# Causal attention with a routed low-rank layer on one core: value blocks issued ahead of the turn's scores

## Chip, core and metric

One core of a Trainium2 chip runs the whole kernel in one launch. The metric is the device time in microseconds; the table below has the median of three runs.

## What is computed

One sequence of 2048 rows of width 128 goes through one layer: layer norm, attention with 16 heads of width 8, and, after a second layer norm, a base product, a shared low-rank branch and six routed low-rank experts of rank 16, of which each row keeps its best two.

```python
qkv = x @ w_qkv                                   # x: [1, 2048, 128], layer-normed
q, k = _apply_rope(q, cos, sin), _apply_rope(k, cos, sin)
scores = jnp.einsum('bhqd,bhkd->bhqk', q, k) * dh ** -0.5
scores = jnp.where(causal, scores, finfo.min)
attn = jax.nn.softmax(scores, axis=-1)
x = x + jnp.einsum('bhqk,bhkd->bhqd', attn, v) ... @ w_out
h = _layernorm(x)
base_out = h @ base_W.T + base_b
shared_out = (h @ shared_A.T) @ shared_B.T
sparse_w = the two largest of softmax(h @ router_W.T + router_b), renormalised
x = x + base_out + shared_out + routed_out        # experts weighted by sparse_w
```

## The kernel before, in words

The attention is computed with scores transposed: keys lie on the partitions, queries on the free dimension. The 16 heads form four groups of four. The queries are cut into six pieces (`PIECES`: 2, 2, 4, 4, 2, 2 tiles of 128), and a piece of one head group is a **group** of work: 24 groups, 23 boundaries between them. For each group the keys are walked from the first to the diagonal.

A **unit** is what fills one score buffer `ps` of 128x1024 (two banks): two heads by 512 queries ("full"), or four heads by 256 ("wide"), with trimmed forms on the diagonal ("ends", "mid", "half"). There are 280 units, and `NS` = 3 score buffers. In the order of units:

- TensorE computes the scores of unit u (`scores`, line 1029) once the exponential of unit u-3 has freed the buffer (line 1020).
- ScalarE takes the exponential of all of it in one instruction (line 625) into one of `NPB` = 8 buffers `pbuf`.
- GpSimd zeroes what lies above the diagonal (line 575), for diagonal units alone.
- TensorE multiplies by the values (`values`, line 1052) into the one accumulator `po`, whose ninth column per head sums the exponentials. This is done by **blocks**, mostly of two units: 145 blocks, block b due `LAG` = 5 turns after its last unit (`blocks_by_unit`). Turns with and without a due block mostly alternate; a unit of kind "mid" is a block by itself and shifts the alternation.
- At a group's last block VectorE transposes `po` out (`evacuate`, line 685), in the block's turn; TensorE's first block of the next group waits for that (line 1048).

Everything else is cut into **jobs**, whose turns are a table (`ORDER`, `PLACES`): T turns normalised rows, Q, K (QS, KS) and V are projections, B is a bound on the scores, and O, X, R, U, F are the output product and the second half of the layer for a chunk of up to four tiles. Each job's product goes through the one bank `pm` and is taken by VectorE (`take`) before the next may start (line 1087). F is two runs of matmuls (lines 1062 and 1119). The rows of the input are prepared in five steps (`PREPS`: 2, 2, 4, 4, 4 tiles) and finished in five (`FINISHES`: 4, 4, 4, 2, 2); for T, Q, K, V and B "chunk n" is the n-th preparation, for O, X, R, U and F the n-th finish, from 0. Where the text names a job it gives the turn: F of chunk 0 is at turn 75, of chunk 1 at 144, of chunk 2 at 199, of chunk 3 (two tiles only) at 253.

Each engine runs its instructions in the order written. TensorE's order is that of the loop at lines 1228 to 1247: in turn u the waits for new keys and queries, then the unit's scores, the filler matmuls of the first four turns, the due block's values, and the jobs. In what follows S, E and V with a number are the scores of a unit, the exponential of a unit, and the values of a block, all counted from 0.

Of the kernel before, what the change touches and what calls it, by code (L numbers as in the profile page):

```python
# [121 lines left out]
def blocks_by_unit():  # L122


    due = {}
    for b, block in enumerate(BLOCKS):
        due.setdefault(block["units"][-1] + LAG, []).append(b)
    return due


def pieces(unit_kind):

    return {"full": [(0, 0, CH, 0)],
            "ends": [(0, P, CH - P, 0), (2, CH - P, P, CH - P)],
            "mid": [(0, 2 * P, 2 * P, 0)],
            "wide": [(0, 0, 2 * P, 0)],
            "half": [(0, P, P, 0)]}[unit_kind]


def pair_step(unit_kind):  # L140

    return P if unit_kind == "half" else 2 * P


def value_terms(block):


    kind = UNITS[block["units"][0]]["kind"]
    terms = []
    for u in block["units"] if kind in ("wide", "half", "mid") else block["units"][:1]:  # L150
        kt, step = UNITS[u]["kt"], pair_step(UNITS[u]["kind"])
        for dk, q0, n, place in pieces(UNITS[u]["kind"]):
            if len(UNITS[u]["pairs"]) == 2:
                sources = [(u, (j % 2) * CH + (j // 2) * step) for j in range(GH)]
            else:
                sources = [(block["units"][j // 2], (j % 2) * CH + place) for j in range(GH)]
            terms.append((kt + dk, q0, n, sources))
    return terms
# [64 lines left out]
def build(nc, x, w_qkv, rope_c, rope_s, w_out, w_down, w_up, w_base, router_b, ident, head_sum,  # L223
# [3 lines left out]
    with ExitStack() as ctx:  # L227
# [196 lines left out]
        def side(stacked, e):  # L424

            return stacked[e * SIDE:(e + 1) * SIDE]
# [7 lines left out]
        def wait_for_fill(engine, p):  # L434

            engine.wait_ge(filled, FILLS_BY_ACT[chunk(p)])
            if FILLS_BY_POOL[chunk(p)]:
                engine.wait_ge(filled_by_pool, FILLS_BY_POOL[chunk(p)])

        def wait_for_keys(engine, p):  # L440

            engine.wait_ge(keys_in[p], 16 * len(SLOTS))

        def wait_for_queries(engine, p):

            if p == 0:
                engine.wait_ge(queries_in[0], 16 * (len(SLOTS) - len(FIRST_BY_POOL) - len(FIRST_BY_ACT)))
                engine.wait_ge(queries_by_pool, 16 * len(FIRST_BY_POOL))
                engine.wait_ge(queries_by_act, 16 * len(FIRST_BY_ACT))
            else:  # L450
                engine.wait_ge(queries_in[p], 16 * len(SLOTS))
# [83 lines left out]
        def _(pool):  # L535
# [23 lines left out]
            for u, unit in enumerate(UNITS):  # L559
                if u in LATE_FILL_UNITS:  # L560
                    stacked, value, tile = LATE_FILLS[LATE_FILL_UNITS.index(u)]
                    fill(kst if stacked == "K" else qst, value, tile, 1)
                if not unit["diagonal"]:
                    continue
                pool.wait_ge(exp_ready, u + 1)
                buf = pbuf[:, u % NPB, :]
                if unit["kind"] in ("mid", "wide"):
                    edges = [buf.rearrange("p (h q) -> p h q", h=4)[:, :, 0:P]]
                elif unit["kind"] == "half":
                    edges = [buf[:, e * CH:e * CH + 2 * P].rearrange("p (h q) -> p h q", h=2) for e in range(2)]  # L570
                else:
                    heads = buf.rearrange("p (h q) -> p h q", h=2)
                    edges = [heads[:, :, place:place + P] for _, _, _, place in pieces(unit["kind"])]
                for edge in edges:
                    ins = nc.gpsimd.affine_select(out=edge, in_=edge, compare_op=ALU.is_ge, fill=0.0, base=0,  # L575
                                                  pattern=[[0, edge.shape[1]], [1, P]], channel_multiplier=-1)
                ins.then_inc(masked, 1)
# [436 lines left out]
        def _(pe):  # L1014
            def scores(u):

                unit = UNITS[u]
                i, g, kt = unit["i"], unit["g"], unit["kt"]
                if u >= NS:
                    pe.wait_ge(exp_ready, u - NS + 1)  # L1020
                if u == 2:
                    pe.wait_ge(second_read, 2)
                for at, pair in enumerate(unit["pairs"]):
                    for dk, q0, n, place in pieces(unit["kind"]):
                        key = (kt + dk) * P
                        q = PIECES[i][0] * P + q0
                        place += at * pair_step(unit["kind"])
                        for e in range(2):
                            ins = nc.tensor.matmul(ps[:, u % NS, e, place:place + n],  # L1029
                                                   side(kst, e)[:, g * 2 + pair, key:key + P],  # L1030
                                                   side(qst, e)[:, g * 2 + pair, q:q + n], start=True, stop=True)
                ins.then_inc(scores_ready, 1)

            def values(b):

                blk = BLOCKS[b]
                last_unit = blk["units"][-1]
                i, g = blk["i"], blk["g"]
                if blk["diagonal"]:
                    pe.wait_ge(masked, MASKS_THROUGH[last_unit])  # L1040
                    pe.wait_ge(v_ready, max(p for at, p in NEW_PREP.items() if at <= i) + 1)
                else:
                    pe.wait_ge(exp_ready, last_unit + 1)
                if blk["first"]:
                    group = i * NG + g
                    pe.wait_ge(v_ready, 2)
                    if group:
                        pe.wait_ge(o_free, group)
                terms = value_terms(blk)
                for m, (kt, q0, n, sources) in enumerate(terms):  # L1050
                    for j, (u, at) in enumerate(sources):
                        ins = nc.tensor.matmul(po[32 * j:32 * j + DH + 1, q0:q0 + n],  # L1052
                                               va[:, kt, g * GH + j, :], pbuf[:, u % NPB, at:at + n],
                                               start=blk["first"] and m == 0,
                                               stop=blk["last"] and m + 1 == len(terms), skip_group_check=True)
                ins.then_inc(block_done, 1)
# [107 lines left out]
            def keep_warm(times, left, right, into=ps[:, 1, 1, :]):  # L1164

                for _ in range(times):
                    nc.tensor.matmul(into, left, right, start=True, stop=True)  # L1167
# [59 lines left out]
            due = blocks_by_unit()  # L1227
            for u in range(len(UNITS)):
                if u in FIRST_UNIT and FIRST_UNIT.index(u) in NEW_PREP:
                    p = NEW_PREP[FIRST_UNIT.index(u)]  # L1230
                    row_maxima(p)
                    wait_for_fill(pe, p)
                    if p == 0:
                        keep_warm(WARM_KEYS, *hot)
                    wait_for_queries(pe, p)
                if u in NEW_KEYS_UNIT:
                    wait_for_keys(pe, NEW_KEYS_UNIT[u])
                scores(u)
                if u < len(WARM_UNITS):
                    keep_warm(WARM_UNITS[u], *hot, pm[:, :])  # L1240
                for b in due.get(u, ()):
                    values(b)
                for n in JOBS_AT.get(u, ()):
                    job(n)
            for u in range(len(UNITS), len(UNITS) + LAG):
# [59 lines left out]
```

## Time and profile before

| what | us |
|---|---|
| median of 3 runs | 309.06 |
| lowest and highest run | 307.85, 311.37 |
| the profiled execution, whole | 307.79 |
| its span, first to last instruction | 306.0 |

The granted TensorE clock was 0.999 of full over the span. A timeline row gives the start in us from the span's start, how long the row's instructions took together, and how many they are (x8); consecutive instructions of one kind are merged. In brackets is the idle time of the engine just before, and what ended it. A row's length includes the draining of its last matmul, so where the next group of TensorE starts is the better measure of what a group costs. Full score groups have two matmuls of 512 columns, wide ones four of 256; a row x4 or x8 can hold two units.

### The profile page before, as it was taken

The numbers are of one execution on the slowest core, as the hardware profiler recorded it, in microseconds if no ns is written. First come the engines' busy times: TensorE is split into PE (matmuls) and PEld (weight loads), VectorE is DVE, ScalarE is ACT, GpSimd is POOL, SyncE is SP. The second block draws the span as 40 slices with busy tenths as digits, with TensorE's granted clock in tenths as the row PEclk, the third lists the DMA queues.
The fourth block names the chain that finished last, engine by engine and source line by source line (L and its number), as shares of the span: only waits on it lengthen the run. The fifth ranks groups of instructions, "written<-read, shape, count | busy, mean of one in ns | idle before, by whom it ended". The sixth has DMA issues, their size and how long they took to land.

```text
span 306.0 us, 7517 instructions
## 1 busy us (share of the span) xinstructions
PE 280.3 (92%) x3008; PEld 101.9 (33%) x3008; DVE 143.4 (47%) x424; ACT 266.2 (87%) x300; POOL 64.0 (21%) x140
## 2 busy tenths in 40 slices
PE   7867887898999899899999999999999999998995
PEld 2613242221423322123324113443533333433352
DVE  6875594689756467936341003761000524101064
ACT  8646597889899789999999999999999999999910
POOL 3673146505032102203012030101101010103000
PEclk9999999999999999999999999999999999999999
DMA  6423147003520100330000100000000000000000
GB/s 206 117 69 95 27 106 209 1 3 81 150 80 2 37 0 1 103 105 2 2 1 2 35 2 2 2 3 0 28 10 3 2 2 0 2 19 2 3 0 17
DMA packets 15704, 11.75 MB, mean 38 GB/s; under 512 B 2081, under 2 KB 14738, under 8 KB 15666
## 3 DMA queue, kind: packets, MB, share of 16 engines
q1 hardware_dynamic: 15170, 10.90, 12.8%
q8 instruction: 25, 0.41, 0.6%
q10 hardware_dynamic: 432, 0.20, 0.3%
q0 software_dynamic: 64, 0.13, 0.2%
q14 instruction: 13, 0.11, 0.1%
HBM read 3.88 MB, written 1.05 MB: 16 GB/s over the span
## 4 chain that ended last, share of the span: by engine, by line
PE 32%; ACT 26%; DVE 21%; issue 16%; DMA 2%; DVEq 1%; SPq 0%; ACTq 0%
ACT pbuf L625 26%; PE po L1052 14%; PE ps L1029 8%; PE pm L1068 3%; DVE rest L703 3%; DVE rot L710 2%; DVE absmax L734 1%; DVE rot L697 1%; DVE rest L720 1%; PE pm L1062 1%; PE pm L1105 1%; DVE parts L727 1%; DVE parts L718 1%; DMA xs<-x_dram 1%; DVE parts L729 1%
## 5 line engine op out<-in xcount | busy, mean ns | idle before, releaser
L625 ACT ACTIVATE pbuf<-ps 128x1024 f32<-128x1024 f32 (+1 forms) x280 | 253.7, 1087 | 21.3 <-PE ps L1029 20.7
L1052 PE MATMUL po<-pbuf,va 128*9 128x256 f32 (+3 forms) x1792 | 143.8, 426 | 4.2 <-DVE oq L685 2.6
L1029 PE MATMUL ps<-qst,kst 64*128 64x256 bf16 (+3 forms) x896 | 96.2, 297 | 6.1 <-ACT pbuf L625 2.1
L575 POOL TENSOR_SCALAR_AFFINE_SELECT pbuf<-pbuf 128x256 f32<-128x256 f32 (+1 forms) x104 | 48.7, 490 | 207.4 <-ACT pbuf L625 205.6
L1029 PEld LDWEIGHTS ps<-qst,kst 64*128 64x128 bf16 x896 | 29.8, 94 | 100.6 <-ACT pbuf L625 75.7
L1052 PEld LDWEIGHTS po<-pbuf,va 128*9 128x9 f32 x1792 | 35.2, 89 | 59.2 <-issue 35.0
L685 DVE STREAM_TRANSPOSE oq<-po 128x256 f32<-128x256 f32 (+1 forms) x24 | 12.9, 539 | 82.2 <-PE po L1052 80.8
L1167 PE MATMUL ps<-kst 128*128 128x512 bf16 x46 | 11.3, 380 | 0.8 <-issue 0.8
L703 DVE TENSOR_TENSOR rest<-pm,sinT 32x512 f32<-32x512 f32 x16 | 11.0, 687 | 0.3
L1068 PE MATMUL pm<-xnT,wqkv 128*128 128x512 f32 x16 | 9.0, 644 | 1.9 <-DVEq L850 1.9
L652 DVE BATCH_NORM_STATS2 stats<-xs 128x6 f32<-128x128 f32 x32 | 7.1, 281 | 2.9 <-DMA xs<-x_dram 1.4
L844 DVE COPY lowT<-pm 113x512 f32<-113x512 f32 (+1 forms) x4 | 2.5, 624 | 12.5 <-PE pm L1115 12.5
L847 DVE TENSOR_TENSOR xs<-pm,xs 128x512 f32<-128x512 f32 (+1 forms) x4 | 2.5, 626 | 11.8 <-PE pm L1119 11.8
L817 DVE TENSOR_TENSOR xs<-pm,xs 128x512 f32<-128x512 f32 (+1 forms) x4 | 2.5, 625 | 9.4 <-PE pm L1105 9.4
L1167 PE MATMUL ps<-xnT 128*128 128x512 bf16 x16 | 5.3, 504 | 1.5 <-DVE xnT L962 1.5
L1167 PEld LDWEIGHTS ps<-kst 128*128 128x128 bf16 x46 | 4.3, 99 | 5.3 <-issue 1.7
L1080 PE MATMUL pm<-hsum,bnd 128*1 128x16 f32 x10 | 1.0, 177 | 5.5 <-DVEq L850 4.4
L710 DVE TENSOR_TENSOR rot<-rot,rest 128x512 f32<-128x512 f32 (+1 forms) x10 | 5.9, 586 | 0.3
L539 POOL MEMSET qst<- 128x512 f32 (+1 forms) x9 | 6.0, 684 | 0.0
L583 ACT COPY kst<-fillers 128x2048 f32<-128x2048 f32 x3 | 5.7, 1896 | 0.0
L720 DVE TENSOR_TENSOR rest<-rot,parts 128x512 f32<-128x512 f32 (+1 forms) x8 | 5.5, 694 | 0.3
L697 DVE TENSOR_TENSOR rot<-pm,cosT 128x512 f32<-128x512 f32 x4 | 2.8, 691 | 5.6 <-PE pm L1068 5.1
(150 smaller groups left out, 183.6 us busy)
## 6 DMA issues: line engine op xcount, KB each, us to landing
qst<-parts SPq DMA_DIRECT2D x18, 128.0 KB, 2.4
kst<-parts SPq DMA_DIRECT2D x18, 128.0 KB, 2.5
xs<-x_dram SPq DMA_DIRECT2D x4, 256.0 KB, 3.5
cosT<-rope_c_dram SPq DMA_DIRECT2D x3, 256.0 KB, 3.9
sinT<-rope_s_dram SPq DMA_DIRECT2D x3, 256.0 KB, 4.3
kst<-parts SPq DMA_DIRECT2D x12, 64.0 KB, 2.1
out_dram<-xs SPq DMA_DIRECT2D x3, 256.0 KB, 2.3
qst<-parts SPq DMA_DIRECT2D x7, 64.0 KB, 2.0
```

What stands on the lines that cost most here:

```text
L539: nc.gpsimd.memset(stacked[:, :, first * P:(first + tiles) * P].bitcast(F32), value).then_inc(filled_by_pool, 1)
L575: ins = nc.gpsimd.affine_select(out=edge, in_=edge, compare_op=ALU.is_ge, fill=0.0, base=0, pattern=[[0, edge.shape[1]], [1, P]], channel_ ...
L625: nc.scalar.activation(probs[:, :, 0:width], ps[:, u % NS, :, 0:width], ACT.Exp, scale=SCALE).then_inc(exp_ready, 1)
L652: ins = nc.vector.bn_stats(stats[:, t, :], xs[:, tile + t, :])
L685: nc.vector.transpose(oq[:, g, mine, :].rearrange("p b r -> p (b r)"), po[:, 0:nt * P]).then_inc(o_free, 1)
L703: ins = nc.vector.tensor_tensor(rest[there:there + HALF, which, cols], product[here:here + HALF, :], sinT[here:here + HALF, c % 2, cols], ...
L710: return nc.vector.tensor_tensor(rot[:, which, cols], rot[:, which, cols], rest[:, which, cols], ALU.add)
L720: then(nc.vector.tensor_tensor(rest[:, which, cols], rot[:, which, cols], parts[:, which, 0, cols], ALU.subtract))
L1029: ins = nc.tensor.matmul(ps[:, u % NS, e, place:place + n], side(kst, e)[:, g * 2 + pair, key:key + P], side(qst, e)[:, g * 2 + pair, q:q ...
L1052: ins = nc.tensor.matmul(po[32 * j:32 * j + DH + 1, q0:q0 + n], va[:, kt, g * GH + j, :], pbuf[:, u % NPB, at:at + n], start=blk["first"] ...
L1068: return nc.tensor.matmul(product, wqkv[:, which, :], xnT[:, chunk(p) % 2, local(p)], start=True, stop=True)
L1167: nc.tensor.matmul(into, left, right, start=True, stop=True)
```

## The change

In a unit's turn the values of the due block are issued ahead of the scores instead of behind them. The jobs stay behind the scores. The waits move with their instructions, and the block due in a turn stands behind the waits for new keys and queries. The orders on VectorE, ScalarE, GpSimd and SyncE are as before.

```diff
                 if u in NEW_KEYS_UNIT:
                     wait_for_keys(pe, NEW_KEYS_UNIT[u])
+                for b in due.get(u, ()):
+                    values(b)
                 scores(u)
                 if u < len(WARM_UNITS):
                     keep_warm(WARM_UNITS[u], *hot, pm[:, :])
-                for b in due.get(u, ()):
-                    values(b)
                 for n in JOBS_AT.get(u, ()):
                     job(n)
```

TensorE around the first group boundary after unit 76, before: V39 (9x256, the last of its group), S81 and S82, V40 (the first of the next), S83 and S84, V41, and T of chunk 4.

```order
L1052 MATMUL po<-pbuf,va 9x256 x4
L1029 MATMUL ps<-qst,kst 128x512 x4
L1052 MATMUL po<-pbuf,va 9x512 x4
L1029 MATMUL ps<-qst,kst 128x512 x4
L1052 MATMUL po<-pbuf,va 9x512 x4
L1095 MATMUL pm<-idf,xn 128x128 x4
L1029 MATMUL ps<-qst,kst 128x512 x4
```

Now, from V39 on:

```order
L1052 MATMUL po<-pbuf,va 9x256 x4
L1029 MATMUL ps<-qst,kst 128x512 x4
L1052 MATMUL po<-pbuf,va 9x512 x4
L1029 MATMUL ps<-qst,kst 128x512 x4
L1052 MATMUL po<-pbuf,va 9x512 x4
L1029 MATMUL ps<-qst,kst 128x512 x2
L1095 MATMUL pm<-idf,xn 128x128 x4
```

The rows between V39 and V40 read alike, but they are S80 and S81 now: S82 and S83 stand behind V40. T, in turn 84, now has one score group between itself and V41.

TensorE around the bound B of chunk 4 in turn 102, before: V50 (the last of its group), S102, B, S103, V51.

```order
L1052 MATMUL po<-pbuf,va 9x256 x4
L1029 MATMUL ps<-qst,kst 128x512 x2
L1080 MATMUL pm<-hsum,bnd 1x16
L1029 MATMUL ps<-qst,kst 128x512 x2
L1052 MATMUL po<-pbuf,va 9x512 x4
```

Now V50 is followed by S101 and S102:

```order
L1052 MATMUL po<-pbuf,va 9x256 x4
L1029 MATMUL ps<-qst,kst 128x512 x4
L1080 MATMUL pm<-hsum,bnd 1x16
L1052 MATMUL po<-pbuf,va 9x512 x4
L1029 MATMUL ps<-qst,kst 128x512 x4
```

S103 has moved behind V51, which waits for the transposition.

TensorE around F of chunk 2 in turn 199, before: V100, S199, F, S200, V101.

```order
L1052 MATMUL po<-pbuf,va 9x256 x8
L1029 MATMUL ps<-qst,kst 128x256 x4
L1062 MATMUL pm<-wbase,feat 128x128 x4
L1119 MATMUL pm<-wup,lowT 128x128 x4
L1029 MATMUL ps<-qst,kst 128x256 x4
L1052 MATMUL po<-pbuf,va 9x256 x8
```

Now V100 is followed by S198 and S199:

```order
L1052 MATMUL po<-pbuf,va 9x256 x8
L1029 MATMUL ps<-qst,kst 128x256 x8
L1062 MATMUL pm<-wbase,feat 128x128 x4
L1119 MATMUL pm<-wup,lowT 128x128 x4
L1052 MATMUL po<-pbuf,va 9x256 x8
L1029 MATMUL ps<-qst,kst 128x256 x4
```

F and V101 are now between S199 and S200, where F alone was.

## Rows read from the trace of the kernel before

**Rows 1.** The page, part 1: busy us (share of span) xinstructions

```profile
PE 280.3 (92%) x3008; PEld 101.9 (33%) x3008; DVE 143.4 (47%) x424; ACT 266.2 (87%) x300; POOL 64.0 (21%) x140
```

**Rows 2.** Table of waits, whole span: us in total, times, longest us

```profile
PEld ps L1029 <- ACT pbuf L625: 75.7, 140, 0.9
ACT pbuf L625 <- PE ps L1029: 20.7, 25, 2.9
PE po L1052 <- DVE oq L685: 2.6, 4, 1.4
```

**Rows 3.** Timeline, 180:200: start, us, engine, instructions [idle before <-releaser]

```profile
179.11 21.82 ACT L625 ACTIVATE pbuf<-ps 128x1024 f32<-128x1024 f32 x24
190.17 1.16 PE L1105 MATMUL pm<-wout,feat 128*128 128x128 f32 x8
191.26 0.39 PE L1029 MATMUL ps<-qst,kst 64*128 64x256 bf16 x4
191.58 1.05 PE L1052 MATMUL po<-pbuf,va 128*9 128x256 f32 x16
192.57 0.61 PE L1029 MATMUL ps<-qst,kst 64*128 64x256 bf16 x8
193.11 1.05 PE L1052 MATMUL po<-pbuf,va 128*9 128x256 f32 x16
```

**Rows 4.** Timeline, 101 to 110 us, after F of chunk 0 and at a group's end

```profile
101.64 0.61 PE L1029 MATMUL ps<-qst,kst 64*128 64x512 bf16 x4
102.07 2.85 ACT L625 ACTIVATE pbuf<-ps 128x1024 f32<-128x1024 f32 x3 [1.89 <-PE ps L1029]
...
106.82 0.72 DVE L685 STREAM_TRANSPOSE oq<-po 128x512 f32<-128x512 f32 x1
107.68 1.04 PE L1052 MATMUL po<-pbuf,va 128*9 128x512 f32 x8 [1.39 <-ACT pbuf L625]
108.66 0.61 PE L1029 MATMUL ps<-qst,kst 64*128 64x512 bf16 x4
109.09 1.94 ACT L625 ACTIVATE pbuf<-ps 128x1024 f32<-128x1024 f32 x2 [0.50 <-PE ps L1029]
```

**Rows 5.** Timeline, 118 to 131 us: K of chunk 4 and the transposition after it

```profile
118.06 1.12 PE L1068 MATMUL pm<-xnT,wqkv 128*128 128x512 f32 x2
...
127.83 0.72 DVE L685 STREAM_TRANSPOSE oq<-po 128x512 f32<-128x512 f32 x1
127.99 0.39 PE L1029 MATMUL ps<-qst,kst 64*128 64x512 bf16 x2
130.11 1.03 ACT L625 ACTIVATE pbuf<-ps 128x1024 f32<-128x1024 f32 x1 [0.37 <-PE ps L1029]
```

**Rows 6.** Timeline, 217 to 222 us: F of chunk 2 in turn 199

```profile
215.42 3.94 ACT L625 ACTIVATE pbuf<-ps 128x1024 f32<-128x1024 f32 x4
217.06 0.39 PE L1029 MATMUL ps<-qst,kst 64*128 64x256 bf16 x4
217.38 1.16 PE L1062 MATMUL pm<-wbase,feat 128*128 128x128 f32 x8
219.36 0.39 PE L1029 MATMUL ps<-qst,kst 64*128 64x256 bf16 x4
219.80 1.03 ACT L625 ACTIVATE pbuf<-ps 128x1024 f32<-128x1024 f32 x1 [0.43 <-PE ps L1029]
221.00 1.51 ACT L625 ACTIVATE pbuf<-ps 128x512 f32<-128x512 f32 x2 [0.17 <-PE ps L1029]
```

**Rows 7.** Timeline, 58 to 63 us: T of chunk 3 and the exponential of unit 37

```profile
58.69 0.65 PE L1095 MATMUL pm<-idf,xn 128*128 128x128 f32 x4 [1.29 <-DVEq L850]
...
62.07 1.02 ACT L625 ACTIVATE pbuf<-ps 128x1024 f32<-128x1024 f32 x1 [1.33 <-PE ps L1029]
```

**Rows 8.** Groups on ScalarE, 100:120, then 120:140: busy, mean ns | idle

```profile
L625 ACT ACTIVATE pbuf<-ps 128x1024 f32<-128x1024 f32 x19 | 18.1, 1039 | 3.4 <-PE ps L1029 3.4
...
L625 ACT ACTIVATE pbuf<-ps 128x1024 f32<-128x1024 f32 x22 | 20.5, 1053 | 0.7 <-PE ps L1029 0.6
```

## Prediction, made before the changed kernel had run

> **What bounds the kernel now.** I read the busy shares first. TensorE is listed at 92% and ScalarE at 87% [rows 1], so neither is plainly the bound. The waits decide: TensorE's weight loads for scores wait 75.7 us in 140 waits for an exponential to free a score buffer, while ScalarE waits only 20.7 us, 25 times, for scores, and TensorE only 2.6 us, 4 times, for a transposition [rows 2]. So the exponentials set the pace nearly everywhere, and the timeline says how fast that is: 24 of them in 21.82 us, 0.91 us each [rows 3]. TensorE needs, for two units and their values, the values (0.99 us from 191.58 to 192.57) and two score groups (0.54, from there to 193.11), together 1.53 us, against 1.82 us of two exponentials [rows 3]. It is ahead by 0.3 us per pair, and a job (O: 1.09 us from 190.17 to 191.26) eats what it gained in four pairs.
>
> I number units 0 to 279 (scores S, exponentials E), blocks of values V 0 to 144; V40 is due at unit 82.
>
> **How much room a score has.** S(u) may start once E(u-3) has ended (I allow 0.1 us for the signal). From a score's start to its exponential's start is 0.43 us (108.66 to 109.09) and such an exponential lasts 1.02 us, as 219.80 with 1.03 shows again [rows 4, 6]. So S(u+1) must start 1.45 us before E(u+1) is due to end, that is at most 4 x 0.91 - 0.1 - 1.45 = 2.1 us after the earliest start of S(u). Between those two starts there is room for the score itself (0.32, from 191.26 to 191.58 [rows 3]) and 1.78 us more: values alone (0.99) or a job alone (1.09) fit; values and a job of 1.09 exceed it by 0.3 us; values and F (F was 217.38 to 219.36, 1.98 us [rows 6]) by 1.2 us. T (0.65 us [rows 7]) and jobs of its size (X, U) fit even with values.
>
> **What the change does.** No instruction is added or removed on any engine, and the orders of VectorE, ScalarE, GpSimd and SyncE, DMAs included, are as before. On TensorE each block of values passes one score group. Seen from the scores this moves the values one gap earlier; seen from the jobs it regroups: before, a job shared its gap with values when both are due in one turn; now, when values are due in the turn after the job. The sum is of what becomes of each such meeting. A block's masks and exponentials are of the unit five turns back and were ready one gap earlier too, so I put the value waits for them at nothing (ScalarE's E(u-4) has ended by then; if POOL were late the block would wait up to one mask).
>
> Up to unit 37 (62 us): 0. Jobs Q, QS and K stand in turns 9, 11 and 13 with values due in 10, 12 and 14, so three exponentials come a value block (0.8 us) later, and V10 now holds back S26. But the end of this stretch is set by VectorE: transposes T of chunk 3 start at 58.69 when its rows are ready, then Q, and E37 starts at 62.07 [rows 7], in both orders. ScalarE idled 1.33 us just before it; that swallows the lateness, at most one value block, that the exponentials carry until then. Bounds: 0 to +0.8.
>
> Units 37 to 83: +1.1 us. Again much is given back, at F of chunk 0: TensorE reaches S76 at 101.64 after an unbroken run of value, job and score [rows 4], and has the same work in front of it in the new order; I keep 0.2 for the wait before U. Then comes the first group boundary behind a long VectorE chain: V39 ends a group and V40 opens the next and must wait for the transposition, which ran from 106.82 to 107.54 because VectorE was on chunk 4's statistics. Before, S81 and S82 had been issued ahead of V40 (107.68; its row names ScalarE, but the transposition ended last) and only E83 was late, by 0.50 us. Now S82 stands behind V40: 107.68 + 0.2 + 0.98 = 108.86, E82 ends at 110.3, E83 at 111.2 against 109.09 + 1.02 = 110.1. So +1.1, of it 0.9 from this wait. Bounds: 0 (if VectorE comes earlier) to 1.9, two exponentials' worth.
>
> Units 84 to 94: 0. T, Q and K of chunk 4 are at turns 84, 86, 92 with values in the same turns. They are relieved, but TensorE arrives late and the walk ends as it began. With 0.32 and 0.21 per score, 0.98 per block, 0.65 for T and 1.05 for Q, K is issued at 118.8, not at 118.06 [rows 5]. Bounds: -1.0, the stalls of these three jobs (3.4 us of the stretch 100 to 120 less 1.89 and 0.50 [rows 4, 8]), to +0.5.
>
> Units 101 to 104: +0.5 us. VectorE's work on K ends 0.7 us later, so the transposition for V50 moves from 127.83 to 128.5 and V51 from 128.7 to 129.4. Before, S103 went ahead of it (127.99) and only E104 idled, 0.37 us [rows 5]. Now S103 starts at 130.4, E103 ends at 131.8, E104 at 132.7 against 131.14: +1.6 in all, 0.5 more than before this place. Bounds 0 to 1.1.
>
> The other meetings, in the room worked out above: V job at 109 relieved (idle 0.6 in the stretch 120 to 140, less 0.37 [rows 8]: about -0.1); O at 114 with V57: +0.3 less a stall that goes, +0.1; R at 127, O at 169, R at 179, and F at 253, which is half as long (two tiles): +0.3 each, 1.2 together; F at 199: 1.2 now and 0.2 for the next score, where before E200 ended at 220.83, 1.47 us after its forerunner at 219.36 (0.56 too late) and the next two 1.68 after it (0.28 too late, one being half as long, 0.49) [rows 6]: 1.4 - 0.84, +0.5; F at 144, which I take to have cost the same before, but where the next score follows 0.2 us behind without loss: 1.2 - 0.84, +0.3. Bounds of these together: 0 (all covered by the lead ScalarE has) to 3.5.
>
> Sum: 0 + 1.1 + 0 + 0.5 - 0.1 + 0.1 + 1.2 + 0.5 + 0.3 = +3.6 us. After unit 83 little can absorb it, since each exponential waits only for the one before, and the last value block waits for the last exponential. The profiled execution took 307.79 us (span 306.0), so it would be 311.4. The three runs shown have a median of 309.06, 1.3 above that execution; on them the forecast is 309.06 + 3.6 = 312.7, and I round it down to 312.5.
>
> A page gives another view of TensorE. By the Trainium skill (Perfetto Trace Analysis, section Identifying the Most-Contended Engine) matmul busy time is no measure of how near TensorE is to its limit, and weight-load busy time is one. That is 33% here [rows 1], so by that rule there would be room for any order, and the time would not change: 309.1. Against it stands the cycle of 1.53 us in 1.82 [rows 3]: five sixths of the time are taken, whatever the weight loads show.
>
> **Rivals.**
> No difference, 309.1 us (308.3 to 310.0): the lead hides the regrouping, as the 1.53 against 1.82 us would let it if no job came close. For it: only 20.7 us of waits in all. Against: F and O meetings are arithmetic on rows.
>
> Not slower, in fact faster, 307.9 us or less: values are now issued while the score waits for its buffer (75.7 us of such waits [rows 2]), so TensorE no longer idles first and lags afterwards. The jobs at 84, 86, 92, 109 and 114 lose their stalls, 1.0 + 0.2 = 1.2 us, and the new meetings cost nothing. It decides if values start more than about 0.3 us earlier than the old ones relative to the exponentials, which covers the excess of 0.3. To pass -1% the early stretch must give some of its idle time too. Against: F exceeds the room fourfold.
>
> Much slower, 319 us: there are 23 group boundaries, and at each the second score after the old group's last block is now behind the transposition (last values end, 0.1, transposition 0.45 to 0.72, first values 0.98). If 17 of them cost 0.6 us each, that is 10 us. Against: two score groups lie between the two value blocks in either order, and the table puts only 2.6 us down to it (V40's 1.39 us come on top).
>
> **Chances.** Forecast 0.50, no difference 0.25, faster-side rival 0.12, much slower 0.13. One per cent, 3.1 us, is about what a measurement of this kernel can tell; the forecast lies just above it. Of its half I put 0.37 above +1% and 0.13 below; of the faster rival 0.07 passes -1%. So faster 0.07, same 0.43, slower 0.50. The range, from the no-difference case's lower part to half way into the last rival, is 308.8 to 317.0; the forecast's own range is 309.8 to 315.5.
>
> **What would show it.** Right: E37 within 0.5 us of 62.07; E82 starting behind V40 and an idle of about 1 us before it; idle of about 1 us before E103, E145 and E200 instead of E104 and the halved pairs; VectorE and the tail (last exponential to end) unchanged in length; ScalarE's wait for scores up from 20.7 to some 24 us plus what the early part shifts. Wrong: if V40 does not hold S82, if the score after F and values follows within 2.2 us, or if the exponentials after 104 us are earlier than before.

## The result, and the profile after

The changed kernel took 312.17 us (median of 4 runs, 310.74 to 313.23) against 308.90 for the kernel before (4 runs, 307.85 to 311.37): 1.0106 times, with a 95% interval of 1.0066 to 1.0145. It is slower by 3.3 us, a third of a microsecond from the forecast of 312.5. The profiled execution took 310.74 us, its span 309.0, against 307.79 and 306.0 before. An execution that is over 1.5% above the fastest of its own kernel stands in no median and no ratio from here on. The agreement is better than the reasons behind it: the order of the instructions costs 2.0 us, not 3.6, and the rest is TensorE's clock, which the prediction did not treat.

The page's busy shares and its row of the granted clock, changed kernel:

```profile
PE 282.4 (91%) x3008; PEld 102.6 (33%) x3008; DVE 142.9 (46%) x424; ACT 266.4 (86%) x300; POOL 64.3 (21%) x140
...
PEclk9999999999999999899999999999999999999999
```

As many instructions as before [rows 1]; TensorE is busy 2.1 us longer with the same matmuls. The clock row has an 8 in its seventeenth slice, about 124 to 131 us.

The table of waits (engine, line, releaser: us in total, times, longest):

```profile
ACT pbuf L625 <- PE ps L1029: 23.9, 27, 3.1
...
PE po L1052 <- DVE oq L685: 3.4, 5, 1.8
```

ScalarE waits 3.2 us more for scores than before (20.7 [rows 2]): that is about the whole difference of the spans, 3.0 us, seen from the engine that sets the pace. The wait for a transposition grew by 0.8 us, in five places, not four.

The timeline at the first group boundary, where V40 now stands ahead of S82 (start, us, engine, instructions):

```profile
106.44 0.72 DVE L685 STREAM_TRANSPOSE oq<-po 128x512 f32<-128x512 f32 x1
...
107.30 1.05 PE L1052 MATMUL po<-pbuf,va 128*9 128x512 f32 x8 [1.75 <-DVE oq L685]
...
108.28 0.60 PE L1029 MATMUL ps<-qst,kst 64*128 64x512 bf16 x4
108.71 1.02 ACT L625 ACTIVATE pbuf<-ps 128x1024 f32<-128x1024 f32 x1 [1.04 <-PE ps L1029]
```

TensorE's idle before V40 has grown from 1.39 to 1.75 us, S82 starts 0.98 us after V40, and ScalarE idles 1.04 us before E82, where before it idled 0.50 us before E83 [rows 4]. V40 itself is 0.38 us earlier than before.

The timeline at B (the bound's sum) and V51, and the busy times of that stretch in steps of 2 us (the columns are window, length, busy of PE, PEld, DVE, ACT, POOL, granted clock, DMA share, GB/s):

```profile
127.91 0.20 PE L1080 MATMUL pm<-hsum,bnd 128*1 128x16 f32 x2 [1.04 <-DVEq L850]
...
128.75 1.89 PE L1052 MATMUL po<-pbuf,va 128*9 128x512 f32 x8 [0.64 <-DVE oq L685]
...
130.57 1.04 PE L1029 MATMUL ps<-qst,kst 64*128 64x512 bf16 x4
131.22 1.94 ACT L625 ACTIVATE pbuf<-ps 128x1024 f32<-128x1024 f32 x2 [2.05 <-PE ps L1029]
```

```profile
126.00:128.00 2.00, 0.96 (x10) 0.28 (x6) 1.84 (x5) 2.00 (x3) 0.00 (x0) 1.00 0.75 203
128.00:130.00 2.00, 1.36 (x10) 0.15 (x8) 1.90 (x5) 1.17 (x2) 0.00 (x0) 0.62 0.44 122
130.00:132.00 2.00, 2.00 (x12) 0.26 (x12) 1.16 (x3) 0.78 (x1) 0.00 (x0) 0.52 0.54 141
```

Here is what nobody forecast. V51 takes 1.89 us where a block takes 1.05, and S103 and S104 take 1.04 where they take 0.61. From 128.5 to 131.9 us the granted clock is half: the lower of its two levels, 1.2 and not 2.4 GHz. It fell within the 0.64 us that TensorE idled for V51, just behind the 1.04 us that it had idled for B. S103 starts 1.82 us after V51 instead of 0.98, and ScalarE idles 2.05 us.

The timeline after F of chunk 2, where V of turn 200 now stands ahead of S200:

```profile
219.75 1.16 PE L1062 MATMUL pm<-wbase,feat 128*128 128x128 f32 x8
...
221.73 1.05 PE L1052 MATMUL po<-pbuf,va 128*9 128x256 f32 x16
...
222.71 0.50 PE L1029 MATMUL ps<-qst,kst 64*128 64x256 bf16 x8
223.15 1.02 ACT L625 ACTIVATE pbuf<-ps 128x1024 f32<-128x1024 f32 x1 [1.03 <-PE ps L1029]
```

F and the values stand in one gap; E200 waits 1.03 us, but the next exponential no longer waits (0.43 and 0.17 before [rows 6]).

Last, T of chunk 3 and E37:

```profile
57.93 0.66 PE L1095 MATMUL pm<-idf,xn 128*128 128x128 f32 x4 [0.34 <-DVEq L850]
...
61.31 1.02 ACT L625 ACTIVATE pbuf<-ps 128x1024 f32<-128x1024 f32 x1 [0.35 <-PE ps L1029]
```

Both are 0.76 us earlier than before (58.69 and 62.07 [rows 7]), though the order on VectorE was not changed.

Where the time went is seen best in the ends of the exponentials, subtracted unit by unit, since each waits only for the one before and for its scores. The middle column is changed minus before. The right one takes instead the kernel changed_filled (below): the same order of work with a few matmuls more that keep the clock at its upper level, so that it shows the order alone.

| unit | changed, us | changed_filled, us |
|---|---|---|
| E37 | -0.76 | -1.01 |
| E76 | -0.38 | -0.63 |
| E85 | +0.27 | +0.03 |
| E100 | +0.35 to 0.44 | +0.11 |
| E104 | +2.02 | +0.79 |
| E116 | +2.29 | +0.78 |
| E147 | +2.67 | +1.16 |
| E172 | +2.87 | +1.35 |
| E203 | +2.96 | +1.44 |
| E279 | +3.08 | +1.56 |

### The profile page after: what moved, and what is told of

It is laid out like the page before. It is cut to its first block, busy times and chain, and to the rows that moved or that the text cites. A ratio compares the mean times of both kernels' runs of the same rounds, so it can differ in the third digit from the quotient of the medians.

```text
span 309.0 us, 7515 instructions
## 1 busy us (share of the span) xinstructions
PE 282.4 (91%) x3008; PEld 102.6 (33%) x3008; DVE 142.9 (46%) x424; ACT 266.4 (86%) x300; POOL 64.3 (21%) x140
## 3 DMA queue, kind: packets, MB, share of 16 engines
HBM read 3.88 MB, written 1.05 MB: 16 GB/s over the span
## 4 chain that ended last, share of the span: by engine, by line
PE 32%; ACT 26%; DVE 21%; issue 18%; DMA 2%; DVEq 1%; SPq 0%; ACTq 0%
ACT pbuf L625 25%; PE po L1052 13%; PE ps L1029 7%; PE pm L1068 3%; DVE rest L703 3%; DVE rot L710 2%; DVE absmax L734 1%; PE pm L1062 1%; PE pm L1105 1%; DVE rot L697 1%; PE pm L1074 1%; DVE stats L652 1%; PE pm L1119 1%; DMA xs<-x_dram 1%; DVE oq L685 1%
## 5 line engine op out<-in xcount | busy, mean ns | idle before, releaser
L625 ACT ACTIVATE pbuf<-ps 128x1024 f32<-128x1024 f32 (+1 forms) x280 | 253.9, 1088 | 24.6 <-PE ps L1029 23.9
L729 DVE TENSOR_TENSOR parts<-rest,parts 128x512 bf16<-128x512 f32 (+1 forms) x8 | 5.3, 667 | 0.3
```

What stands on the lines that cost most here:

```text
L625: nc.scalar.activation(probs[:, :, 0:width], ps[:, u % NS, :, 0:width], ACT.Exp, scale=SCALE).then_inc(exp_ready, 1)
```

## The experiments

Theory A, as predicted: order alone, +3.6 us, in the terms listed. Theory B, formed on the trace above: order costs less, and TensorE's longer idles bring the clock down more often. "At full clock" means executions whose mean granted clock was 0.997 or more, and a time given for them is their mean; the kernel before, measured beside every experiment, took 307.87 us at full clock (28 executions). In the edits `ahead` chooses per turn whether the due block goes in front of the scores:

```diff
-                for b in due.get(u, ()):
+                ahead = u != 103
+                for b in due.get(u, ()) if ahead else ():
                     values(b)
                 scores(u)
...
+                for b in () if ahead else due.get(u, ()):
+                    values(b)
```

**v51_back.** The changed kernel, with V51 behind S103 as before (the edit above).

> The changed kernel, but in turn 103 alone the score goes ahead of V51 again, as before. Theory: of the 3.1 us that the changed trace lost by its last exponential, 1.7 us are lost at this one place, because S103 stands behind V51 and because TensorE, idle before B and before V51, has its clock halved for 3.4 us. Then this kernel takes about 1.0 to 1.7 us less than the changed one (about 310.5 us), its clock in the profile stays at full through 124 to 134 us, and E103 is not late. Rival (many equal small losses, all boundaries alike): at most 0.2 us is regained.

Measured: 310.01 us against 308.97, 1.0046 (1.0025 to 1.0067). That is 2.2 us less than the changed kernel's 312.17 (2.7 less than its 312.74 when it was run again, below), where 1.0 to 1.7 were expected. In its trace the exponentials lose 0.1 us from E102 to E114, where the order alone costs 0.5 (from changed_filled) and the profiled changed kernel lost 1.7. But five of its twelve executions ran at full clock and took 309.73, and the two such executions of the changed kernel took 309.64: at like clock V51's place makes no difference that these few executions show. Nearly all of the gain is that the clock fell less often. It fell here too, at another place; the stretches of the trace:

```profile
24.00:26.00 2.00, 2.00 (x26) 0.79 (x24) 0.78 (x3) 1.51 (x2) 0.53 (x1) 0.50 0.42 106
26.00:28.00 2.00, 1.95 (x24) 0.82 (x22) 1.27 (x3) 1.47 (x2) 1.20 (x4) 0.50 0.34 86
```

TensorE had idled 2.25 us for B in turn 3, an idle that all these kernels share, the one before among them.

**firsts_back.** The changed kernel, but a block that is the first of its group stays behind the scores.

```diff
+                ahead = not any(BLOCKS[b]["first"] for b in due.get(u, ()))
```

> The changed kernel, with the scores ahead of the values wherever the due block is the first of its group (23 boundaries and the first group). Theory of two places (V40 and V51 behind a long VectorE chain): about 0.9 + 1.7 = 2.5 us less than the changed kernel, within 1 us of the kernel before. Theory that all boundaries cost: no more than that can be there, since the trace shows idle only at E82 and E103; a gain above 3 us would speak for it. Rival (only the meetings of jobs and values cost): less than 0.5 us regained.

Measured: 309.66, 1.0048 (1.0023 to 1.0072); at full clock 308.82 (3 of 11). That is 0.9 above before at like clock and 0.8 to 1.1 below the changed order. So the first blocks of all groups together carry about 1 us of order, and the rest 1 us; there is no room for the 10 us of the "much slower" rival.

**early_only.** The change in turns 0 to 37 alone.

```diff
+                ahead = u < 38
```

> The change made in turns 0 to 37 alone. Theory: VectorE's chain to T of chunk 3 sets E37, so the time is that of the kernel before, within 0.5 us, although three exponentials near 30 to 38 us start 0.8 us later. Rival (the early idle on ScalarE is lost time that nothing absorbs): 1 us or more slower than before.

Measured: 307.48, 0.9961 (0.9945 to 0.9976); seven of twelve at full clock, 307.27, which is 0.6 below before's 307.87. Theory A said nothing would be left of this stretch; it gains, clear of the noise. The median is 1.5 us below the 308.97 of the kernel before beside it, and the part beyond 0.6 is the clock, which stayed full in seven of twelve executions against eight of 34. The cause of the 0.6 is looked at under the unexpected findings.

**warm_103.** The changed kernel with five matmuls more that compute nothing used: two ahead of B, three ahead of V51.

```diff
                 for b in due.get(u, ()):
+                    if u == 103:
+                        keep_warm(3, *hot, ps[:, 103 % NS, 0, :])
                     values(b)
...
+                if u == 102:
+                    pe.wait_ge(exp_ready, 101)
+                    keep_warm(2, *hot, ps[:, 103 % NS, 0, :])
```

> The changed kernel in its new order, with five filler matmuls (128x512) into the free score buffer on TensorE: two ahead of B in turn 102, three between B and V51. Theory that the halved clock is a good part of the loss at V51: the clock stays at full there, V51 is followed by S103 after 0.98 us and not 1.82, and the kernel takes 0.8 to 1.2 us less than the changed one. Rival (the order alone costs it): the clock may stay up, but the time is within 0.3 us of the changed kernel's.

Its timeline at V51:

```profile
131.09 1.04 PE L1052 MATMUL po<-pbuf,va 128*9 128x512 f32 x8
...
132.07 0.61 PE L1029 MATMUL ps<-qst,kst 64*128 64x512 bf16 x4
132.50 1.94 ACT L625 ACTIVATE pbuf<-ps 128x1024 f32<-128x1024 f32 x2 [1.05 <-PE ps L1029]
```

V51 takes 1.04 us again and ScalarE waits 1.05, not 2.05: half of that wait was the clock, half the order. The median was 311.35 (1.0067, 1.0041 to 1.0093), 0.8 us under the changed kernel's 312.17, at the lower end of what was expected; four of eleven executions were at full clock, with 309.93. Other places were left: in this trace the clock was half for 6.8 us from 25.1 us on, again behind turn 3.

**changed_again.** The changed kernel once more, with its own neighbours.

> The changed kernel once more, to see its granted clock over many executions. Theory that the idle of TensorE before B and V51 brings a halved clock of its own, beside those that all kernels here share: fewer executions at full clock than the kernel before has (8 of 34) and more with two or three halvings, median near 312.0 us. Rival (the halvings belong to the executions and not to the order): the same shares of clocks as before, and at like clock 2.4 us or more above it.

Measured: 312.74, 1.0110 (1.0071 to 1.0148), nearly the same ratio as the first time (1.0106). Its profiled execution shows the other boundary at half clock (timeline, then stretches):

```profile
107.28 1.70 PE L1052 MATMUL po<-pbuf,va 128*9 128x512 f32 x8 [1.76 <-DVE oq L685]
...
109.56 1.94 ACT L625 ACTIVATE pbuf<-ps 128x1024 f32<-128x1024 f32 x2 [1.93 <-PE ps L1029]
```

```profile
108.00:110.00 2.00, 2.00 (x16) 0.25 (x12) 1.55 (x5) 0.44 (x1) 0.00 (x0) 0.50 0.00 0
...
132.00:134.00 2.00, 2.00 (x12) 0.14 (x11) 0.76 (x2) 1.78 (x2) 0.00 (x0) 0.50 0.72 186
```

V40 takes 1.70 us, not 1.05, and E82 waits 1.93, not 1.04. The same program thus lost its clock behind V40 and V51 here, and behind V51 alone in the first profile. Over 13 executions of the changed kernel that give a clock, two were at full clock (309.64 us), one had a mean of 0.994 (310.74) and ten had less (means 312.5 for the three of the first time, 312.9 for the seven of the second). At full clock the new order costs 309.64 - 307.87 = 1.8 us. Of the kernel before, 28 of 97 were at full clock (307.87), 55 lost about as much as one such stretch (median 309.0) and 14 more (309.3 to 311.4).

**meetings_only.** The kernel before, with the values ahead in only the seven turns where the prediction saw a job and values meet.

```diff
+                ahead = u in (115, 128, 145, 170, 180, 200, 254)
```

> The kernel before, with values ahead of the score only in the seven turns that follow a job of turns 114, 127, 144, 169, 179, 199 and 253. Theory of the room of 2.1 us: each meeting costs what the changed trace shows there (0.2, 0.1, 0.4, 0.2, 0.1, 0.3, 0.2 us), together 1.3 to 1.8 us at like clock. Rival (the lead hides them): under 0.4 us.

Measured: 311.53, 1.0100 (1.0061 to 1.0139), and 311.48 in the four of six executions at full clock: +3.6 at like clock. That is twice what was expected, and over four times what the same seven turns cost inside the full change (+0.8 from E104 to E279). The seven terms of the prediction, 2.1 us with O at turn 114, lie between the two: what a meeting costs depends on where the blocks around it stand. The timelines at O of turn 114 show how, first this kernel, then the changed one:

```profile
137.48 1.05 PE L1052 MATMUL po<-pbuf,va 128*9 128x512 f32 x8
138.46 0.39 PE L1029 MATMUL ps<-qst,kst 64*128 64x512 bf16 x2
138.77 1.16 PE L1105 MATMUL pm<-wout,feat 128*128 128x128 f32 x8
139.86 1.05 PE L1052 MATMUL po<-pbuf,va 128*9 128x512 f32 x8
...
141.28 2.85 ACT L625 ACTIVATE pbuf<-ps 128x1024 f32<-128x1024 f32 x3 [0.73 <-PE ps L1029]
```

```profile
138.94 1.05 PE L1052 MATMUL po<-pbuf,va 128*9 128x512 f32 x8
139.92 0.61 PE L1029 MATMUL ps<-qst,kst 64*128 64x512 bf16 x4
140.46 1.16 PE L1105 MATMUL pm<-wout,feat 128*128 128x128 f32 x8
141.54 1.04 PE L1052 MATMUL po<-pbuf,va 128*9 128x512 f32 x8
...
142.96 2.85 ACT L625 ACTIVATE pbuf<-ps 128x1024 f32<-128x1024 f32 x3 [0.35 <-PE ps L1029]
```

Between S114 and S115 lie O and V57 in both, 2.4 us. But here V56 lies in front of S114 (one group, 138.46), while in the full change V56 went ahead of S113, and S113 and S114 follow each other (139.92, x4). Measured from the end of E111, which frees the buffer, S114 starts 0.66 us later here (137.80, 138.46) and 0.33 in the full change (139.86, 140.19). ScalarE has those 0.3 us more of lead when the long gap begins: 0.35 us of wait, not 0.73. The other six meetings were not read in this way.

**bounds_only.** The kernel before, with values ahead in turns 82 and 103 alone.

```diff
+                ahead = u in (82, 103)
```

> The kernel before, with values ahead of the score only in turns 82 and 103. Theory: a score held behind a value block that waits for VectorE costs 0.9 us at E82 and 0.5 us at E103 (more where the clock halves there), together 1.0 to 1.6 us at like clock. Rival (boundaries cost nothing by themselves): under 0.4 us.

Measured: 310.54, 1.0057 (1.0021 to 1.0094). The three at full clock took 308.94, +1.1; the five with the lowest clock 312.08 (mean). Two blocks moved out of 145 cost 1.1 us of order where theory A put 1.4 (0.9 + 0.5), and they cost clock: the median lies 1.6 above the executions at full clock, where the kernel before beside it (308.82, 307.87) has 0.9. In the profile E82 waits 2.12 us behind a clock that fell at 109.5 us.

**before_warm.** The kernel before, with nine filler matmuls more in turn 3.

```diff
-WARM_UNITS = (2, 2, 2, 2)
+WARM_UNITS = (2, 2, 2, 11)
```

> The kernel before, with nine more filler matmuls (128x512) in turn 3, where TensorE idles 2.3 us before the second B. Theory that this idle stretch is where many executions lose their clock for a while (two profiles show it halved for 6.8 us from 23.0 and 25.1 us): nearly all executions run at full clock and the median falls from 309.0 to about 307.9 us. Rival: the clock falls elsewhere or by chance, and the shares stay as they are.

Measured: 307.91, 0.9965 (0.9942 to 0.9989), all twelve executions at full clock, between 307.64 and 308.25. The timeline of that place:

```profile
20.83 2.55 PE L1167 MATMUL pm<-kst 128*128 128x512 bf16 x10
23.31 0.20 PE L1080 MATMUL pm<-hsum,bnd 128*1 128x16 f32 x2
```

The idle in front of B is filled, and B starts without a wait. So the kernel before lost 1.0 us in most runs to this one idle.

**changed_filled.** The changed kernel, all three idles filled: the nine in turn 3, five ahead of V40, two ahead of B and three ahead of V51.

```diff
+                    if u == 82:
+                        pe.wait_ge(exp_ready, 80)
+                        keep_warm(5, *hot, ps[:, 82 % NS, 0, :])
```

> The changed kernel with filler matmuls wherever its profiles show TensorE idle ahead of a halved clock: nine more in turn 3, five ahead of V40 in turn 82, two ahead of B and three ahead of V51. Theory that what the changed order costs beside 1.8 us of order is its clock: all executions at full clock, near 309.7 us, 3 us under the changed kernel's median and 1.8 over the kernel before at like clock. Rival (fillers cost as much as the clock gives, or other idle takes their place): above 311 us or clocks below 0.995 in many executions.

Measured: 309.92, 1.0041 (1.0023 to 1.0059), twelve of twelve at full clock. Its timeline at V40:

```profile
105.87 1.03 PE L1167 MATMUL ps<-kst 128*128 128x512 bf16 x4 [0.57 <-ACT pbuf L625]
...
107.06 1.05 PE L1052 MATMUL po<-pbuf,va 128*9 128x512 f32 x8 [0.16 <-DVE oq L685]
...
108.04 0.60 PE L1029 MATMUL ps<-qst,kst 64*128 64x512 bf16 x4
...
108.47 1.94 ACT L625 ACTIVATE pbuf<-ps 128x1024 f32<-128x1024 f32 x2 [1.04 <-PE ps L1029]
```

E82 waits 1.04 us, as predicted, with the clock out of the way. Against before_warm, also at full clock throughout, the new order costs 309.92 - 307.91 = 2.0 us (309.32 to 310.60 against 307.64 to 308.25). The same comparison without fillers, from the few executions at full clock, gave 1.8. The clock is the rest: the changed kernel's medians of 312.17 and 312.74 lie 2.3 and 2.8 above 309.92, those of the kernel before beside them 1.0 and 0.9 above 307.91, so the clock adds 1.3 and 1.9 to the differences measured, 3.3 and 3.9. Theory B stands.

**early_warm, early_jobs_warm, mended.** Three tries at the best of both, all with the nine fillers in turn 3: the change in the early turns; there and at the jobs of turns 54, 84, 86, 92 and 109, which the prediction said it would relieve; and everywhere but the seven meetings and, from turn 38, the first blocks.

```diff
+                ahead = u < 38
+                ahead = u < 38 or u in (54, 84, 86, 92, 109)
+                ahead = u not in (115, 128, 145, 170, 180, 200, 254) and (u < 38 or not any(BLOCKS[b]["first"] for b in due.get(u, ())))
```

> Values ahead of the score in turns 0 to 37 alone, and nine more fillers in turn 3. Theory (two gains that add up: VectorE's casts are no longer slowed beside GpSimd's masks, 0.6 us; the clock stays full, 1.1 us in most executions): median 307.2 to 307.4 us, the best so far, 1.6 us under the kernel before. Rival (the second gain is in the first already): 307.5 us or more, no better than the early change alone.

> The same, and values ahead of the score also in turns 54, 84, 86, 92 and 109, where a job of the same turn follows. Theory of relief (values run while the score waits for its buffer): 0.5 to 1.2 us less than without them, about 306.5 us. Rival (the work before the next score is the same, so nothing is gained, and the two blocks in neighbouring gaps make the score of the turn itself late): within 0.2 us of it or slower.

> Nine more fillers in turn 3, and values ahead everywhere but in the seven turns after a job and, from turn 38 on, in the turns whose block is the first of its group. Theory: without the places that were found to cost, the new order is as good as the old one: at full clock within 0.3 us of the early change with fillers (307.3 us). Rival (switching the order back and forth makes new tight gaps): 1 us or more above that.

| kernel | median, us | ratio (95%) | at full clock, us | of 12 |
|---|---|---|---|---|
| early_warm | 307.46 | 0.9963 (0.9941 to 0.9985) | 307.03 | 7 |
| early_jobs_warm | 307.27 | 0.9969 (0.9951 to 0.9987) | 307.28 | 11 |
| mended | 308.49 | 0.9998 (0.9979 to 1.0018) | 308.49 | 11 |

At full clock early_warm is 0.8 under before (307.87). Its ratio is that of early_only (0.9961), and seven of twelve at full clock are as many as there: the nine fillers are not seen to add to the early change, which is nearly what the rival said. The five jobs add nothing: their stalls were moved, not removed (the one of turn 54 fell from 0.62 to 0.39 us, those near 84 and 86 changed places). Mended is 1.2 to 1.5 above them, where at most 0.3 was expected. In its trace E58 waits 1.04 us, where it waits 0.66 in the full change, and E202 waits 0.71, where neither the kernel before nor the changed one waits at all: the mixed order has narrow places of its own, as the rival said, though they were not tested one by one. The fillers of turn 3 do not always save the clock: in the profile of early_warm it was half from 17.7 us on, ahead of them.

```profile
18.00:20.00 2.00, 2.00 (x8) 0.41 (x7) 1.27 (x3) 0.19 (x1) 0.30 (x1) 0.50 0.04 12
```

The best kernels of the study are early_jobs_warm, early_warm and early_only, with medians of 307.27, 307.46 and 307.48, 1.2 to 1.5 us under the kernel before beside each. The fillers alone (before_warm) came to 307.91.

## Why the prediction was right, and where it was not

The time (312.5 for 312.17), the direction and the range were right. By its own steps, with changed_filled as the measure of order, since it is free of the clock:

- **Up to unit 37: 0.** Wrong, and outside its bounds of 0 to +0.8: -0.8 to -1.0 us. The step took T of chunk 3 as fixed by VectorE "in both orders". T came at 57.93, not 58.69. The step let the masks move with the exponentials and never asked whether VectorE's instructions beside them keep their length; they did not (last section).
- **Units 37 to 83: +1.1.** 37 to 76 gave +0.4 for a forecast of 0.2, and V40 +0.7 for 0.9. The mechanism is as told: S82 behind V40, 1.04 us of idle. Two things around it were off: V40 was 0.38 us earlier, and the clock fell behind V40 in one of the changed kernel's two profiles.
- **Units 84 to 94: 0.** Right: from E85 to E100 the difference moved by about 0.1. K stands at 118.02, not at 118.8 (118.06 before), since the 0.76 us gained early offset the lateness that was forecast for it.
- **Units 101 to 104: +0.5.** Right for the order (+0.7 from E100 to E104 here, +0.5 by E114, where v51_back has 0.1, so about 0.4 is V51's place), and less than a third of what the profiled changed kernel shows, +1.7, the rest being the halved clock. This is the term that was missing. The prediction spoke of this very wait and its length, and of what it holds back, but never asked what an idle TensorE does to its own clock.
- **V job at 109 and O at 114: 0 together**; measured 0 (0.3 in the profiled changed kernel). **R at 127, O at 169, R at 179, F at 253: +1.2 together**; measured 0.1 + 0.2 - 0.1 + 0.2 = 0.4. **F at 144: +0.3**, measured 0.3. **F at 199: +0.5**, measured 0.2. The room rule named the right exponentials (E145 and E200 wait where it said), but it took an overrun of 0.3 us as a loss of 0.3, and the four such meetings lost 0.1 each on average. Room was counted for one gap alone, from a score that starts as early as it may. The two timelines of meetings_only show that the gap before it counts too: the same meeting cost more there, where S114 started later.
- **Sum.** The terms after unit 37 come to 2.6 us (from -1.01 to +1.56) for a forecast of 3.6, those before to -1.0 for 0; so +1.6 in the traces and +2.0 in the medians. The clock added 1.3 to 1.9. That the total came within 0.3 us is luck: an order term 1.6 to 1.8 too large and a clock term that was missing cancelled.

On what would show it: E37 missed its half microsecond by 0.26. ScalarE's wait (23.9 for 24), the idles before E82, E103, E145 and E200 of about 1 us and the unchanged tail came as said, that before E103 only with the clock held.

The rivals: "no difference" is excluded by both ratios. "Faster" was right only about the early stretch, and for another reason; the relief at the jobs it named did not show. "Much slower" fails on firsts_back. By the rule of the Trainium skill (Perfetto Trace Analysis, section Identifying the Most-Contended Engine), which the prediction weighed, 33% of weight-load busy time would leave room; that share stayed at 33% while the order cost 2.0 us. The measurement decides: the share says nothing of how narrow single places are.

Not settled: why one execution loses its clock at a given idle and the next does not, whether the 0.4 us of order at V51, seen in the traces, is there in the times, and why the fillers, which held the clock of before_warm in all twelve executions, did so in only seven of early_warm.

## What to carry to other kernels

When work that waits on another engine is put in front of work that is ready, two costs come: the ready work is late, and the engine idles longer; on TensorE the second can cost nearly as much as the first, through the clock (here 1.3 to 1.9 us beside 2.0). Before comparing two orders, list the clock of every execution and compare at like clock, or fill the idles with matmuls that compute nothing; here nine of them gave the kernel before 1.0 us. Judge the room of a score with the gap before it in view, and test a stretch alone before calling it fixed by another engine.

## What the runs showed of the hardware that was not expected

**The clock.** Idles of 1.75 us (V40), of 1.04 and 0.64 us (B and V51) and of 2.25 us (turn 3) each came with a stretch at 0.50 of full clock, begun in the idle or just behind it, in some profiles and not in others: at V40 in those of changed_again and bounds_only, not in the first one of the changed kernel; at V51 in both of the changed kernel, not in that of bounds_only; at turn 3 in three (v51_back, warm_103, bounds_only), not in that of the kernel before. One such stretch cost 1 us or slightly more: a block of values 1.70 to 1.89 us for 1.05, two score groups 1.04 for 0.61. The kernel before has mainly two levels of time, 307.9 and 309.0 us; with the idle of turn 3 filled it had one.

**VectorE beside GpSimd.** In the early stretch the casts of K and its remainder changed their length without any change to them. VectorE and GpSimd, timeline at 38 to 58 us, kernel before:

```profile
38.55 1.99 POOL L575 TENSOR_SCALAR_AFFINE_SELECT pbuf<-pbuf 128x512 f32<-128x512 f32 x3 [5.79 <-ACT pbuf L625]
38.58 0.88 DVE L718 CAST parts<-rot 128x512 bf16<-128x512 f32 x1
...
45.62 0.64 POOL L575 TENSOR_SCALAR_AFFINE_SELECT pbuf<-pbuf 128x512 f32<-128x512 f32 x1 [1.98 <-ACT pbuf L625]
45.64 0.90 DVE L727 CAST parts<-rest 128x512 bf16<-128x512 f32 x1
...
57.09 1.49 DVE L421 TENSOR_SCALAR xn<-xs,mv,rstd 128x128 f32<-128x128 f32 x4
```

and the changed kernel:

```profile
38.74 0.43 DVE L718 CAST parts<-rot 128x512 bf16<-128x512 f32 x1
...
39.69 1.60 POOL L575 TENSOR_SCALAR_AFFINE_SELECT pbuf<-pbuf 128x512 f32<-128x512 f32 x3 [5.43 <-ACT pbuf L625]
...
40.41 0.61 DVE L727 CAST parts<-rest 128x512 bf16<-128x512 f32 x1
...
45.66 0.43 DVE L727 CAST parts<-rest 128x512 bf16<-128x512 f32 x1
...
46.81 0.64 POOL L575 TENSOR_SCALAR_AFFINE_SELECT pbuf<-pbuf 128x512 f32<-128x512 f32 x1 [2.43 <-ACT pbuf L625]
...
56.62 1.20 DVE L421 TENSOR_SCALAR xn<-xs,mv,rstd 128x128 f32<-128x128 f32 x4
```

A cast that starts together with a mask takes 0.88 or 0.90 us, one with no mask beside it 0.43. All fourteen traces agree: the 101 casts of this shape with no mask beside them took 0.41 to 0.43 us, the 67 with one 0.51 to 0.90. The new order makes the exponentials, and so their masks, 1.1 us later here, and two casts of the chain that ends in T escape them.

How that becomes 0.76 us at T has to be followed step by step. The first escape (38.74) is worth nothing in the end: the next cast now meets the mask (0.61 for 0.43), and the cast behind it starts at 44.47, 44.45 before. The second (45.66) saves 0.47, of which 0.32 reach the statistics of chunk 3's rows (53.52 for 53.84). The other 0.44 come right ahead of T: the last step of the row scale takes 0.16 us for 0.31 and the four scalings of the rows (L421) 1.20 for 1.49, with the masks beside them again 0.6 us later (57.21 for 56.64). In early_only the casts are as in the changed kernel, but the statistics wait 0.48 us for rows of x from DRAM, and T is only 0.30 us earlier than before (58.39).

It fits what the Trainium skill says (VectorE: DVE Perf Modes, section Two Vector instructions with no wait between them), that a single-source instruction in a two-port mode reads through an SBUF interface shared with GpSimd; no trace shows in which mode a cast ran. That casts beside masks are slower is seen in every trace. But no run moved the masks alone, so that this is the cause of the early gain is argued, not shown.
